# Two attentions first, then two feed-forwards over each quantised weight tile

## The chip, the cores and the metric

The kernel runs on one core of one Trainium2 chip. A core has TensorE (PE, matrix products), VectorE (DVE), ScalarE (ACT), GpSimd (POOL) and SyncE (SP), which here only issues DMAs; each has a queue of its own and works through it in order. The metric is the device time of one execution in microseconds, the median of several runs.

## The reference

One layer over an input of 4 x 1024 rows of 512 float32 values:

```python
# x: (4, 1024, 512)
x = x + layernorm(attn(layernorm(x), W_qkv, W_out))
x = x + layernorm(ffn(layernorm(x), w_gate_up, w_proj))

# attn: 16 heads of 32, element by element
q, k, v = split(x @ W_qkv.T); q, k = elu(q) + 1, elu(k) + 1
out = q * cumsum(k * v) / (q * cumsum(k) + 1e-9)        # sums along the 1024 rows
attn = out @ W_out.T * 32 ** -0.5

# ffn: both weights ternary: groups of 64, scale = mean|w|, w = round(w / scale) clipped to -1..1, times scale
h = silu(x @ Wgate.T) * (x @ Wup.T)                      # 2048 wide
ffn = rms_norm(h) @ Wproj.T
```

The straight-through form `w + (w_hat - w)` is computed in bfloat16 and its rounding is kept.

## The kernel before, in words

The 4096 rows are cut into 8 chunks of 512 (N); two chunks make a batch element, and an odd chunk takes its running sums (`carry`) from the even one. Attention and its weights work in float32 split in a high and a low part (`_hi`, `_lo`), three products per group of 4 x 128 rows of depth, 12 matmuls each: `group(s, g)` for g = 0 to 11 gives q, k and v of the four head tiles j (g = 3j + part), and `project_att(s, t)` projects the attention's result. The hidden layer has 16 tiles m of 128 (MT): `gate_up(f, m)` is 16 matmuls, `project(f, k)` adds hidden tile k into four banks with 8 matmuls, three tiles behind (LAG).

All engines run the same schedule, each written out by hand in its own block, and they meet at semaphores. `start()` does chunk 0 and 1's attentions, all weight preparation and the feed-forward of chunk 0. After it `step(s)` does the attention of chunk s and the feed-forward of chunk s - 1: 12 groups, the transposes of the normalised x1 (L470), 16 gate and up tiles with projections, then in `close` the transposes of the next chunk (L424) and the attention's output projection (L532). Steps 2 to 5 are a loop with a register (`run_steps`), 6 to 8 are written out.

Attention on the other engines, for a head tile j: ScalarE makes relu and exp (`features`, L737, L738), DVE combines them (L1087, L1089), multiplies k by v (L1097) and makes two running sums (L1106, L1109), together `front`. POOL (`numden`, L897 to L902) makes denominator and numerator, DVE the reciprocal (L1120, `back_reciprocal`), the quotient (L1128, `back_output`) and, after ScalarE's high part (L745), the low part (L1134, `back_lo`).

In the feed-forward, for a tile m: ScalarE applies silu (L768), DVE multiplies by the up product (L1171, `hidden_value`), ScalarE takes the high part (L779), DVE the remainder (L1176, `hidden_lo`), ScalarE squares (L785) and POOL adds the squares (L933, `add_square`).

The quantised weights come in 24 batches (BATCHES), 16 of gate and up rows ("gu") and 8 of the projection. A batch is 128 x 1024 and passes: load of two halves (SP, L358, three buffers), cast to bfloat16 (ACT, L692), `scale` (DVE, L1003 to L1011: sums of magnitudes, scale, reciprocal), `divide` (POOL, L866, four parts), `ternary` (DVE, L1030, L1032: clip and round), `scale_back` (POOL, L873, four parts), `diff` (DVE, L1038), from batch 13 on `total` (DVE, L1044), `transpose_weights` (PE, L447) into banks 2 and 3, and `put` (ACT, L701 and L704). PE turns weight and difference, 16 small matmuls, or from batch 13 (SUMMED) the one total, 8. Every two "gu" batches `row_scales` makes powers of two by masks on the exponent. `beside(m)` says which batches are turned beside tile m of chunk 0's feed-forward: seven are done before it, one per tile after that, two at tile 11. In this feed-forward gate and up have one bank each (`single=0`).

The order around a tile in `start()` on DVE is, for example, `hidden_value(0, m)`, `diff(b + 1)`, `hidden_lo(0, m)`, `total(b + 1)`, `ternary(b + 2)`, `scale(b + 3)`, and on POOL

```python
add_square(0, m)
for b in beside(m):
    scale_back(b + 2), divide(b + 3)
```

## Time and profile before

| | us |
|---|---|
| median of 3 runs | 1216.65 (1215.43 to 1217.48) |
| the profiled execution | 1217.18 |
| its span in the trace | 1215.0 |
| PE busy | 1107.6 (91%) |
| DVE busy | 808.3 (67%) |
| POOL busy | 555.6 (46%) |
| ACT busy | 444.5 (37%) |

The busy shares are over the whole span; the page also gives them in 40 slices of 30 us, in tenths:

```profile
PE   6859747877999999999989999999999999899997
DVE  6999989984787358843786268744785278535423
POOL 2856787784543424442442434342544253215322
PEclk9889888988999999999999999999999999999999
```

The first ten slices are `start()`, and the rest are steps. PEclk is the granted TensorE clock in tenths of full speed, 9 being 90% or more. A line of the timeline gives start, duration, engine, line, operation, output <- input, and in brackets how long the engine sat idle before and who released it.

### The profile page before, as it was taken

To read this page: it belongs to the slowest core of one execution; us is meant where nothing else is said; L and a number is where in the kernel's file an instruction comes from. 1 tells how busy PE (TensorE), PEld (TensorE's weight loads), DVE (VectorE), ACT (ScalarE), POOL (GpSimd) and SP (SyncE) were. 2 spreads that over 40 slices of the span, in tenths; PEclk is the share of its full clock that TensorE was granted. 3 is DMA by queue.
4 is the path that set the end of the run, shared out by engine and by line. 5 is a ranking of instruction groups with operands and counts; after the bars stand their busy time and mean duration, and the time that the engine had idled before them with its cause. 6 is when DMAs were issued, how large, how long until landed. Compare 5 with 4: busy or idle time off the path is not lost. (4 is left out here: it accounts for less than half of the span.)

```text
span 1215.0 us, 15144 instructions
## 1 busy us (share of the span) xinstructions
PE 1107.6 (91%) x5288; PEld 656.4 (54%) x5288; DVE 808.3 (67%) x1243; ACT 444.5 (37%) x754; POOL 555.6 (46%) x612
## 2 busy tenths in 40 slices
PE   6859747877999999999989999999999999899997
PEld 5648523334854477446844486446844585454443
DVE  6999989984787358843786268744785278535423
ACT  4423444543244323342234323441344314433432
POOL 2856787784543424442442434342544253215322
PEclk9889888988999999999999999999999999999999
DMA  7301121210210021000210021000200020100000
GB/s 253 102 1 53 36 68 45 95 44 1 70 35 1 1 70 35 1 1 2 71 35 1 1 70 35 1 1 10 90 6 1 1 70 1 35 1 1 35 1 35
DMA packets 28026, 42.92 MB, mean 35 GB/s; under 512 B 1328, under 2 KB 9520, under 8 KB 27952
## 3 DMA queue, kind: packets, MB, share of 16 engines
q1 hardware_dynamic: 27952, 41.95, 10.5%
q8 instruction: 45, 0.74, 0.2%
q14 instruction: 29, 0.24, 0.1%
HBM read 33.55 MB, written 8.39 MB: 35 GB/s over the span
## 5 line engine op out<-in xcount | busy, mean ns | idle before, releaser
L487 PE MATMUL bank<-x3t,wgu_t 128*128 128x512 f16 x1792 | 412.7, 384 | 28.1 <-DVE ht L1171 14.6
L487 PEld LDWEIGHTS bank<-x3t,wgu_t 128*128 128x128 bf16 x1792 | 173.8, 99 | 248.2 <-DVE ht L1171 20.2
L933 POOL TENSOR_TENSOR acc<-acc,ht 128x512 f32<-128x512 f32 x120 | 152.7, 1273 | 329.1 <-ACT ht L785 328.9
L494 PE MATMUL bank<-wproj_t,hid 128*128 128x512 bf16 x1024 | 242.2, 382 | 7.9 <-DVE tr L1097 7.5
L459 PE MATMUL bank<-xnt,wqkv_hi 128*128 128x512 f32 x768 | 196.6, 399 | 9.9 <-DVE tr L1097 9.4
L1171 DVE TENSOR_TENSOR ht<-ht,bank 128x512 f32<-128x512 f32 x128 | 86.5, 676 | 172.9 <-PE bank L487 135.6
L494 PEld LDWEIGHTS bank<-wproj_t,hid 128*128 128x128 f16 x1024 | 100.4, 98 | 128.8 <-DVE tr L1097 8.0
L459 PEld LDWEIGHTS bank<-xnt,wqkv_hi 128*128 128x128 f32 x768 | 146.2, 192 | 40.3 <-issue 10.3
L779 ACT ACTIVATE hid<-ht 128x512 f16<-128x512 f32 x128 | 80.5, 629 | 214.1 <-DVE ht L1171 214.1
L1176 DVE TENSOR_TENSOR hid<-ht,hid 128x512 f16<-128x512 f32 x128 | 105.8, 827 | 71.6 <-ACT hid L779 71.5
L785 ACT ACTIVATE ht<-ht,grow 128x512 f32<-128x512 f32 x120 | 86.6, 722 | 124.4 <-DVE hid L1176 124.4
L897 POOL TENSOR_TENSOR tk<-tq,ts 128x512 f32<-128x512 f32 x32 | 64.9, 2027 | 133.2 <-DVE ts L1106 133.2
L1120 DVE RECIPROCAL tk<-tk 128x512 f32<-128x512 f32 x32 | 106.9, 3340 | 10.5 <-POOL tk L900 10.5
L459 PE MATMUL bank<-xnt,wqkv_lo 128*128 128x512 f32 x384 | 104.4, 394 | 0.0
L768 ACT ACTIVATE ht<-bank 128x512 f32<-128x512 f32 x128 | 74.8, 585 | 31.7 <-PE bank L487 31.6
L459 PEld LDWEIGHTS bank<-xnt,wqkv_lo 128*128 128x128 f32 x384 | 73.5, 191 | 15.7
L532 PE MATMUL bank<-wout_hi,outt 128*128 128x512 f32 x256 | 69.6, 404 | 4.4 <-DVE outt L1134 4.4
L737 ACT ACTIVATE tr<-bank 128x512 f32<-128x512 f32 x32 | 19.2, 598 | 134.6 <-PE bank L459 121.9
L745 ACT ACTIVATE outt<-tr 128x512 fp32r<-128x512 f32 x32 | 19.9, 623 | 109.6 <-DVE tr L1128 109.6
L487 PE MATMUL bank<-x3t_last,wgu_t 128*128 128x512 f16 x256 | 57.5, 379 | 0.0
L532 PEld LDWEIGHTS bank<-wout_hi,outt 128*128 128x128 f32 x256 | 48.2, 190 | 15.6 <-issue 4.9
L879 POOL TENSOR_TENSOR vecf<-vecf,columns 128x4 f32<-128x4 f32 x8 | 8.1, 1018 | 80.5 <-DVE vecf L1060 80.5
(166 smaller groups left out, 1323.6 us busy)
## 6 DMA issues: line engine op xcount, KB each, us to landing
raw_q<-in_L_ffn_w_gate_up_dram SPq DMA_DIRECT2D x32, 256.0 KB, 2.8
xn<-in_L_attn_x_dram SPq DMA_DIRECT2D x7, 1024.0 KB, 5.1
x<-in_L_attn_x_dram SPq DMA_DIRECT2D x7, 1024.0 KB, 6.3
out_dram<-xn SPq DMA_DIRECT2D x7, 1024.0 KB, 8.7
raw_q<-in_L_ffn_w_proj_dram SPq DMA_DIRECT2D x16, 256.0 KB, 2.9
raw_a<-in_L_attn_W_qkv_dram SPq DMA_DIRECT2D x4, 768.0 KB, 9.1
xn<-in_L_attn_x_dram SPq DMA_DIRECT2D x4, 256.0 KB, 3.7
raw_out<-in_L_attn_W_out_dram SPq DMA_DIRECT2D x1, 1024.0 KB, 13.1
```

Of the source, the lines that this page charges most:

```text
L459: last = pe.matmul(bank[:], w[:, k, rows], xnt[:, part_x, k], start=(n == 0), stop=(n == 3 * KD - 1))
L487: last = pe.matmul(bank[:], wgu_t[:, k, first_row:first_row + P], x[:, part, k], start=(n == 0), stop=(n == 2 * KD - 1))
L494: last = pe.matmul(ps[4 + t][:], hid[:, part, k % HR, t * P:(t + 1) * P], wproj_t[:, k], start=(k == 0 and part == 0), stop=(k == MT - 1 a ...
L532: last = pe.matmul(bank[:], outt[:, part_o, k, t * P:(t + 1) * P], w[:, k], start=(n == 0), stop=(n == 3 * KD - 1))
L768: act.activation(ht[:, m % 2], ps[gate_bank(single, m)][:], ACT.Silu, scale=1.0 / SCALE3).then_inc(silu_done, 1)
L779: act.activation(hid[:, 0, m % HR], ht[:, m % 2], ACT.Copy).then_inc(h_hi, 1)
L785: act.activation(ht[:, m % 2], ht[:, m % 2], ACT.Square, scale=grow[:, m:m + 1]).then_inc(sq_done, 1)
L897: pool.tensor_tensor(tk[:, d], tq[:, d], ts[:, d], ALU.mult).then_inc(den_mul, 1)
L933: pool.tensor_tensor(acc[:], acc[:], ht[:, m % 2], ALU.add).then_inc(acc_done, 1)
L1120: dve.reciprocal(tk[:, d], tk[:, d]).then_inc(rec_done, 1)
L1171: dve.tensor_tensor(ht[:, m % 2], ht[:, m % 2], ps[gate_bank(single, m) + 1][:], ALU.mult).then_inc(h_done, 1)
L1176: dve.tensor_tensor(hid[:, 1, m % HR], ht[:, m % 2], hid[:, 0, m % HR], ALU.subtract).then_inc(h_lo, 1)
```

## The change

Only `start()`, what it calls and the storage are changed; steps 3 to 8 do the same work in the same order, but for one thing: three of the groups of step 3 are done ahead (AHEAD), and the steps are all written out.

- The attentions of chunks 0 and 1 are done first, both to the end: chunk 1's output projection is no longer beside the third chunk's.
- Of the weight batches only 0 and 1 are turned before the first gate. Batches pass a ring of 6 places that lies on freed attention storage (RING); divide and scale are four batches ahead of the turning, scale back and ternary two.
- The feed-forwards of chunks 0 and 1 run together: tile m of chunk 0 and tile m - 4 of chunk 1 (BEHIND). Tiles 0 to 3 of chunk 0 stand alone, one batch each; tiles 4 to 15 have two batches (m even) or one (m odd); then four tiles of chunk 1 alone with the transposes of chunk 2. The gate and up products of both rotate over three banks (`UNIT_AT`), and all turned halves go through bank 3.
- Chunk 0's projections are four tiles behind. Chunk 1's hidden tiles are all kept (`hid_b`), and their projections are done in `attention_of_third`: eight of them before the groups of chunk 2, the others one behind each of the first eight groups.
- Chunk 1's x1 is stored to the output's place in DRAM and loaded back later. The load of chunk 3's x waits for the store of chunk 0.
- Nothing is summed any more (`total` and SUMMED go); every batch is turned with 16 small matmuls. `row_scales` makes the power of two by float arithmetic, five dependent operations instead of three.

```diff
-        BEFORE = 7
-        SUMMED = 13
-        TWICE = (11,)
...
+        TURNED = {0: [2], 1: [3], 2: [4], 3: [5]}
+        for m in range(BEHIND, MT):
+            n = TURNED[m - 1][-1] + 1
+            TURNED[m] = [n, n + 1] if m % 2 == 0 else [n]
...
+        UNITS = []
+        for m in range(MT + BEHIND):
+            for f, n in ((0, m), (1, m - BEHIND)):
+                UNITS += [(f, n, which) for which in range(2) if 0 <= n < MT]
+        UNIT_AT = {unit: i for i, unit in enumerate(UNITS)}
+
+        def unit_bank(f, m, which):
+
+            return ps[UNIT_AT[f, m, which] % 3]
...
         def run_steps(eng, step):
-            with eng.Fori(1, NC // 2 - 1) as i:
-                step(2 * i, Step(2))
-                step(2 * i + 1, Step(3))
-            for s in range(NC - 2, NC + 1):
+            for s in range(3, NC + 1):
                 step(s, Step(s))
...
+            sp.wait_ge(y_ready, NT)
+            sp.wait_ge(kept_x1, 16)
+            sp.dma_start(x1[:], out_ch[1]).then_inc(back_x1, 16)
+            sp.dma_start(out_ch[0], xn[:]).then_inc(stored, 16)
+            sp.wait_ge(stored, 16)
+            sp.dma_start(xn[:], x_ch[3]).then_inc(x_loaded, 16)
...
+            def transpose_half(b, i):
+                kind, m = BATCHES[b]
+                turned = ident_b[:]
+                if i == 0:
                     pe.wait_ge(q_diff, b + 1)
...
+                    pe.wait_ge(q_out, 2 * b + i)
...
+                    for part, w in enumerate(PLACES[b]):
+                        last = pe.matmul(ps[3][:, n * P:(n + 1) * P], w[:, cols], turned, start=(part == 0), stop=(part == 1))
...
+            def attention_of_second():
...
+                    group(1, g, start=True)
+                    if g == 6:
...
                             project_att(0, t)
...
+                pe.wait_ge(ln2_x, NT)
+                transpose_x1(0, lambda k: None)
+                pe.wait_ge(att_hi, 2 * KD)
+                pe.wait_ge(att_lo, 2 * KD)
+                for t in range(NT):
+                    wait_group_read(pe, 1, 8 + t)
+                    project_att(1, t, ps[4 + t])
...
+                for m in range(BEHIND, MT):
+                    first, last = TURNED[m][0], TURNED[m][-1]
+                    project(0, m - BEHIND)
+                    unit(0, m, 0)
+                    transpose_half(first, 0)
+                    unit(0, m, 1)
+                    if last > first:
+                        transpose_half(first, 1)
+                    unit(1, m - BEHIND, 0)
+                    transpose_half(last, int(last == first))
+                    unit(1, m - BEHIND, 1)
+                    if last > first:
+                        transpose_half(last, 1)
...
+            def attention_of_third():
...
+                square_sums(0)
+                half = range(MT // 2)
+                for k in half:
+                    wait_hid(1, k)
+                    for t in range(NT - 1):
...
+                        project_tile(1, k, t)
...
+                square_sums(1, NT)
+                pe.wait_ge(ss_read, 2)
+                for k in half:
+                    project_tile(1, k, NT - 1).then_inc(FF_SECOND["pr_done"], 1)
+                for g in range(NG):
...
+                    group(2, g, start=True)
+                    k = MT // 2 + g
+                    if k < MT:
+                        wait_hid(1, k)
+                        for t in range(NT):
+                            last = project_tile(1, k, t)
...
+                for k in range(KD):
+                    wait_group_read(pe, 2, 8 + k)
+                transpose_x(3, bank=lambda k: ps[4 + k])
...
+                for g in range(AHEAD):
+                    group(3, g)
...
+                for t in range(NT):
+                    pe.wait_ge(fin_x, at(NT, 1, t))
+                    project_att(2, t)
...
+                for m in range(BEHIND, MT):
+                    first, last, n = TURNED[m][0], TURNED[m][-1], m - BEHIND
+                    hidden_gate(1, m), put_half(first, 0), hidden_hi(1, m)
+                    if last > first:
+                        put_half(first, 1)
+                    hidden_gate(2, n), put_half(last, int(last == first)), hidden_square(1, m), hidden_hi(2, n)
+                    if last > first:
+                        put_half(last, 1)
+                    hidden_square(2, n)
+                    for b in TURNED[m]:
+                        turn_and_cast(b)
...
+                for m in range(BEHIND, MT):
+                    b = TURNED[m][0]
+                    scale_back_and_divide(b)
                     add_square(0, m)
...
+                    if TURNED[m][-1] > b:
+                        scale_back_and_divide(b + 1)
+                    add_square(1, m - BEHIND)
...
+            def tile(s, j):
+
+                d = (s, j + 1) if j < KD - 1 else (s + 1, 0)
+                back_reciprocal(s, j)
+                front_features(*d), front_products(*d, True)
+                back_output(s, j)
+                front_sums(*d, d[0] % 2 == 1)
+                back_lo(s, j)
...
+                for m in range(BEHIND, MT):
+                    n, b = m - BEHIND, TURNED[m][0]
+                    hidden_value(0, m)
+                    if b + 1 < NBATCH:
+                        diff(b + 1)
+                    hidden_lo(0, m)
+                    if b + 2 < NBATCH:
+                        ternary(b + 2)
+                    hidden_value(1, n), scale_from(b + 4), hidden_lo(1, n)
+                    if TURNED[m][-1] > b:
+                        diff(b + 2)
...
+                            ternary(b + 3)
+                        scale_from(b + 5)
```

## Rows read from the trace of the kernel before

**Rows 1.** Busy time by stretch: us, engines' busy (instructions), granted clock, DMA.

```profile
0.00:145.08 145.08, 108.84 (x560) 88.77 (x561) 129.90 (x196) 53.49 (x103) 89.02 (x118) 0.92 0.27 89
145.08:297.17 152.09, 108.30 (x562) 50.29 (x561) 127.44 (x194) 70.11 (x128) 120.01 (x155) 0.88 0.17 54
312.52:445.52 133.00, 131.37 (x617) 77.72 (x616) 84.53 (x130) 47.61 (x78) 52.23 (x51) 1.00 0.08 24
219.82:243.33 23.51, 19.25 (x103) 8.57 (x101) 21.56 (x34) 12.35 (x23) 20.67 (x27) 1.00 0.38 124
```

**Rows 2.** The same for POOL lines L866, L873 and L933, in this order.

```profile
219.82:243.33 23.51, 10.59 (x12) 1.00 0.38 124
219.82:243.33 23.51, 6.44 (x12) 1.00 0.38 124
219.82:243.33 23.51, 3.83 (x3) 1.00 0.38 124
```

**Rows 3.** Timeline of PE: start, us, line, operation.

```profile
78.79 3.75 PE L459 MATMUL bank<-xnt,wqkv_hi 128*128 128x512 f32 x8 [9.38 <-DVE tr L1097]
...
293.27 0.61 PE L447 MATMUL bank<-ident_b,yq_own 128*128 128x128 bf16 x8
...
400.81 3.62 PE L487 MATMUL bank<-x3t,wgu_t 128*128 128x512 f16 x16
...
406.00 3.62 PE L487 MATMUL bank<-x3t,wgu_t 128*128 128x512 f16 x16
...
445.52 1.98 PE L459 MATMUL bank<-xnt,wqkv_hi 128*128 128x512 f32 x8
...
448.25 1.98 PE L459 MATMUL bank<-xnt,wqkv_hi 128*128 128x512 f32 x8
```

**Rows 4.** Timeline of DVE in the start and in step 2.

```profile
27.07 2.48 DVE L995 TENSOR_TENSOR wout_lo<-bank,wout_hi 128x512 fp32r<-128x512 f32 x4 [0.42 <-ACT wout_hi L682]
...
304.47 2.48 DVE L1051 BATCH_NORM_STATS2 stf<-bank 128x6 f32<-128x512 f32 x4
...
318.06 0.69 DVE L1087 SCALAR_TENSOR_TENSOR tq<-tq,tr 128x512 f32<-128x512 f32 x1 [3.66 <-ACT tq L738]
...
336.95 1.22 DVE L1106 TENSOR_TENSOR_SCAN ts<-columns,tk 128x512 f32<-128x512 f32 x1
...
341.21 3.35 DVE L1120 RECIPROCAL tk<-tk 128x512 f32<-128x512 f32 x1 [1.74 <-POOL tk L900]
...
348.80 0.68 DVE L1087 SCALAR_TENSOR_TENSOR tq<-tq,tr 128x512 f32<-128x512 f32 x1
...
350.79 1.22 DVE L1106 TENSOR_TENSOR_SCAN ts<-columns,tk 128x512 f32<-128x512 f32 x1
```

**Rows 5.** Waits of PE in step 2: us in total, times, longest.

```profile
PE bank L487 <- ACT ht L768: 1.6, 2, 1.2
```

**Rows 6.** Timelines of DVE (first two) and POOL, single operations.

```profile
195.17 0.68 DVE L1128 TENSOR_TENSOR tr<-tq,tk 128x512 f32<-128x512 f32 x1
...
196.38 0.42 DVE L1030 TENSOR_SCALAR yq_xn<-yq_xn 128x1024 bf16<-128x1024 bf16 x1
...
209.25 2.32 POOL L866 TENSOR_TENSOR yq_own<-wb_own,grs 128x256 bf16<-128x256 bf16 x4
...
228.11 3.67 POOL L866 TENSOR_TENSOR yq_set<-wb_set,grs 128x256 bf16<-128x256 bf16 x4
```

**Rows 7.** Groups of DVE lines from 219.82 to 243.33.

```profile
L1171 DVE TENSOR_TENSOR ht<-ht,bank 128x512 f32<-128x512 f32 x4 | 2.6, 650 | 0.0
...
L1176 DVE TENSOR_TENSOR hid<-ht,hid 128x512 f16<-128x512 f32 x3 | 2.9, 961 | 0.4 <-ACT hid L779 0.4
...
L1044 DVE TENSOR_TENSOR yq_own<-yq_own,wb_own 128x1024 bf16<-128x1024 bf16 x2 | 2.2, 1097 | 0.0
```

**Rows 8.** Waits of POOL from 219.82 to 243.33.

```profile
POOL yq_set L873 <- DVE yq_set L1032: 1.6, 2, 0.8
```

**Rows 9.** DMA issues: count, KB each, median us to landing.

```profile
out_dram<-xn SPq DMA_DIRECT2D x7, 1024.0 KB, 8.7
```

More of the change, by code:

```diff
@@ L416, in transpose_raw, with transpose_x @@
                     done.then_inc(wa_t, 1)
-            def transpose_x(c):
-                for k in range(KD):
+            def transpose_x(c, tiles=range(KD), bank=lambda k: ps[k]):
+                for k in tiles:
                     for t in range(NT):
@@ L458, in group @@
                     for k in range(KD):
-                        last = pe.matmul(bank[:], w[:, k, rows], xnt[:, part_x, k], start=(n == 0), stop=(n == 3 * KD - 1))
+                        last = pe.matmul(bank[:], w[:, k, rows], xnt_of(s)[:, part_x, k], start=(n == 0), stop=(n == 3 * KD - 1))
                         n += 1
@@ L471, in transpose_x1, with gate_up_unit, gate_up @@
                     last.then_inc(t3_done, 1)
-            def gate_up(f, m, single=MT, start=False, x=x3t):
-                for which, first_row, done in ((0, m * P, gate_done), (1, FF + m * P, up_done)):
-                    bank = ps[gate_bank(single, m) + which]
+            def gate_up_unit(bank, x, m, which):
+                first_row = which * FF + m * P
+                for n in range(2 * KD):
+                    part, k = divmod(n, KD)
+                    last = pe.matmul(bank[:], wgu_t[:, k, first_row:first_row + P], x[:, part, k],
+                                     start=(n == 0), stop=(n == 2 * KD - 1))
+                return last
+            def gate_up(f, m, single=MT, x=x3t):
+                q, c = ffn(f)
+                for which in range(2):
                     if m == 0 and which == 0:
@@ L481, in gate_up @@
                     if before >= 0:
-                        pe.wait_ge(h_done if which else silu_done, at(MT, f, before))
-                    if start:
-                        pe.wait_ge(q_out, 2 * (GU_AT[m] + 1))
-                    for n in range(2 * KD):
-                        part, k = divmod(n, KD)
-                        last = pe.matmul(bank[:], wgu_t[:, k, first_row:first_row + P], x[:, part, k],
-                                         start=(n == 0), stop=(n == 2 * KD - 1))
-                    last.then_inc(done, 1)
@@ L520, in square_sums @@
                     pe.wait_ge(x3t_lo, KD * (s + 1))
-                pe.wait_ge(acc_done, (MT - 1) * s)
-                for t in range(NT):
-                    last = pe.matmul(ps[3][:, t:t + 1], acc[:, t * P:(t + 1) * P], ones[:], start=True, stop=True)
-                last.then_inc(ss_done, 1)
+                square_sums(s - 1)
             def project_att(s, t, bank=None):
@@ L771, in hidden_parts @@
[L771 to L785 removed]
+                hidden_hi(s, m)
@@ L1283, in start @@
-                close(1, Step(1))
+                split_weights(4, 4 * KD)
+                front(0, 0, False, True), stats_x(1)
+                tile(0, 0), split_x(1), tile(0, 1), tile(0, 2), tile(0, 3), tile(1, 0)
+                stats_att(0)
+                back_reciprocal(1, 1), add_ln2(0), front_features(1, 2), front_products(1, 2, True)
+                back_output(1, 1), front_sums(1, 2, True), back_lo(1, 1)
+                stats_x1(0), scale(0), scale(1)
+                tile(1, 2), x3_lo(0), ternary(0), scale(2)
@@ new lines, in start @@
+                add_final(0)
+                read_square_sums(1, NT)
+                front(2, 0, False, True)
+                tile(2, 0), tile(2, 1), stats_x(3), tile(2, 2)
+                split_x(3, bank=lambda k: ps[4 + k])
+                stats("f", 1, lambda t: ps[t][:], before_second)
+                back_reciprocal(2, 3)
+                dve.wait_ge(back_x1, 16)
+                add_final(1, first_bank=0)
+                back_output(2, 3), back_lo(2, 3)
+                stats_att(2)
```

660 lines of the change are left out of this document (376 added, 284 removed).

## The prediction

> **What bounds the kernel now.** Read the page's busy shares first, then one line per stage: TensorE (PE) is busy for 131.4 of 133.0 us in the step from 312.52 to 445.52, at a granted clock of 1.00, but for 108.8 of the first 145.1 us and 108.3 of the next 152.1 us, at 0.92 and 0.88 [rows 1]. So after 297 us only PE's work counts, and before it some 80 us of PE time are empty. In those two stages VectorE (DVE) is busy 129.9 and 127.4 us; GpSimd (POOL) 120.0 us in the second. The reader is to see that the change can win in the first 300 us alone, and only as far as DVE and POOL can be spread over PE work.
>
> In the middle of the first feed-forward (219.82 to 243.33, three weight batches and three tiles) POOL is busy 20.7 of 23.5 us, DVE 21.6, PE 19.3 [rows 1]. POOL's lines there: dividing 10.59, scaling back 6.44, squares 3.83 us [rows 2]. One batch takes 23.51 / 3 = 7.84 us.
>
> The milestone for comparing: the moment when the third attention's output projection is done. Before, it ends at 445.52, where the next step's first of 12 groups starts [rows 3]. After, three of these groups are done by then: 12 matmuls take 448.25 - 445.52 = 2.73, 0.227 each, so they are 8.2 us, so PE is level at 445.5 + 8.2 = 453.7. But DVE counts too: it opened the step before this one at 318.06, 5.5 us after 312.52, held up by groups and activations [rows 4]; with three groups already there it opens 1.5 us after the milestone (my choice: its statistics' tail). DVE is level if the milestone comes at 451.0 - 1.5 = 449.5. PE waits in a steady step for 1.6 us only, at the first tiles, where DVE and ScalarE are late [rows 5], so the later of the two decides: level is 449.5.
>
> **Stage A, two attentions without quantisation.** Nothing up to the last weight split at 27.07 + 2.48 = 29.5 depends on what was moved [rows 4]. Then DVE alone: first head's front 5.0, statistics 3.1 (four of 0.6 and the small ones [rows 4]), first tile 9.2, split of x 2.4: 49.2. A tile in steady state: from the first scan's start to the reciprocal 341.21 - 336.95 = 4.26 (the 1.74 us of waiting for POOL's denominator in it stays, as nothing is left to fill it), reciprocal 3.35, output 0.7 [rows 6], features and product 350.79 - 348.80 = 2.0, less overlaps: 10.1 us [rows 4]. Bounds: 9.3 without any wait, 10.3 without overlap. The second tile's scan ends at 56.2, three more end at 86.4, tail 2.1: 88.5. Attention statistics, reciprocal, residual, the next head: 14.5, 103. Statistics 3.1, two scales 4.6, a tile 10, split of x3 2.4: 123. A list of 19 us (five parts of quantisation, reciprocal 3.35, output and split) puts the last attention split at 135, ternary(3) at 142. POOL's two divides and its denominator fit beside it. PE: 48 matmuls of 0.227 are 10.9 us, plus 2 for the slow clock after a long idle (8 matmuls took 3.75 instead of 1.98 us after 9.38 us idle, at 78.79 [rows 3]): 148. The two first batches then pass one bank by halves: four rounds of 8 small matmuls at 0.056 (0.45) [rows 3] and a copy of 0.6 with its hand-overs, 1.3 to 1.6 us each. First gate at 153.4. Before, it started at 145, but with two heads and an output projection still to do.
>
> **Stage B1, four tiles of the first chunk alone.** Four batches, second residual and its normalisation. DVE per tile and batch: 21.56 / 3 = 7.2 [rows 1], without the sum of 1.1 [rows 7] 6.1, and 0.3 more for the row scales (five dependent small operations where three were, every other batch): 6.4. Four of these, two statistics of 3.1, a residual 2.7, x3's remainder 2.4 and a first wait of 2 for the gates: some 38. POOL has four divides (3.5 each), four scalings (2.15), four squares, and 4.4 and 3.2 us for normalisation and residual: 39. End near 192. PE needs 17 us of this.
>
> **Stage B2, twelve iterations: two tiles, 1.5 batches and one projection each.** PE: 24 matmuls took 406.00 - 400.81 = 5.19, so 0.216 each [rows 3]; 32 + 8 of them 8.65, 24 small ones 1.35: 10.0 us. DVE: 2 x (0.65 + 0.96) = 3.2 for two tiles [rows 7], and 1.5 batches of 6.4 - 1.6 = 4.8: 10.4. POOL: 1.5 x (10.59 + 6.44)/3 + 2 x 1.28 = 11.1 [rows 2]. In 219.82 to 243.33 POOL's idle (2.8 of 23.5 us) is mostly the round divide - ternary - scale back (two of its three waits there are 1.6 us [rows 8]); the change puts divide four batches ahead instead of three, and this goes. But even iterations (two batches) cost POOL 13.9 and odd ones 8.2, where PE then sets 9.6; the queues let little slack pass (three rotating banks), so between 11.1 and (13.9 + 9.6)/2 = 11.8 I take 11.7. Bounds: PE's 10.0 below, 12.5 above (POOL keeping its wait of 0.93 per batch). Nine iterations until the divides run out: 105; normalisation of the third chunk 5 on POOL; three iterations at PE's pace 30. End 332 to 335. Four last iterations of one tile, projection and transpose: 22.7. End 357.5.
>
> The extra 8 small matmuls of the 11 batches whose halves are no longer summed (88 x 0.056 = 4.9 us of PE) stand under POOL's pace but for the last four batches (1.8); the sums' 11 x 1.1 us leave DVE, which is second. ScalarE has 12.35 us of work in 23.51 [rows 1], 4.1 per batch and tile, so at most 8.2 per iteration of 11.7: covered.
>
> **Stage C, third attention.** Split of the last x tile behind the last value: PE waits 1.5. Square sums 0.8, 24 pairs of projections 10.4, square sums and their read 1.2, 8 pairs 3.5: 17.4. Twelve groups of 2.72 and eight projections of 1.73 alternate to 63.8. DVE's third tile, behind the chunk statistics, gives its product at 68.8, and the transposes of the fourth chunk wait for it: 5 us. Transposes 2, split of x behind the tile's end at 72.7: groups start at 75.2, a 4 us wait. Three groups, partly at the slow clock, 84.5; DVE in that time statistics, reciprocal, final residual and the last head: 86.3. Projection 10.9: 97.2. (Bounds 88, if the split slips in early, and 101.) The fourth chunk's load comes after a store whose copies land 8.7 us after issue [rows 9]; x is due at 60 and the chain ends near 35: hidden.
>
> Milestone 357.5 + 97.2 = 454.7, 5.2 later than 449.5. The profiled span becomes 1215.0 + 5.2 = 1220.2; the execution took 1217.18, 0.5 more than the median of 1216.65, so 1216.65 + 5.2, rounded down for B2's choice near its upper bound: **1221 us**. Unrolling the loop gives nothing: the looped step from 312.52 to 445.52 already has PE at 131.4 of 133.0.
>
> **A rule weighed against the trace.** In the three batches above, DVE and POOL operations that touch both buffers slow each other: a divide of four parts takes 3.67 us, and 2.32 undisturbed [rows 6]. The Trainium skill (SBUF — State Buffer, "SBUF: two separate sides") says that the pair of ports shared by the two is held exclusively for a whole instruction, by a GpSimd operation or by a VectorE one with two SBUF inputs or in a two-port mode. Added up by that rule from undisturbed durations (POOL 2.32 + 2.32 + 1.27 = 5.9; DVE 0.85 for a ternary and three of 0.68, 2.9 [rows 6]) a batch would need 8.8 us, and the trace shows 7.84: the lock is real but doesn't cover whole durations.
>
> **Rivals.** (1) *PE's pace holds in B2.* If divides and ternaries shrink to undisturbed durations (1.5 x 4.64 + 2.6 = 9.5 us of POOL), the two queues slip past one another and an iteration is 10.0 to 10.3: 9 x 1.5 = 14 less, and B1 two less: 1205. For it: 2.32 us divides occur. Against it: DVE is at 10.4 itself, so they will meet. (2) *The shared port sums up.* By POOL 9.5 and DVE 1.5 x 1.53 + 2 x 0.68 = 3.7 us an iteration is 13.1: 9 x 1.4 = 13 more: 1234. Against it the 7.84. The skill's rule named above is this case. (3) *The start's waits chain.* The single bank for transposes ties PE, ScalarE and DVE in B1 and B2: every half waits for a copy, and a late difference stops the gates behind it on PE's queue; at 1 us per iteration this is 12 to 20 us: 1235. (4) *The third attention hides everything*, stage C at 88: 1212.
>
> **Chances.** Forecast 0.42, (1) 0.28, (2) and (3) 0.20, (4) 0.10. Against no change 0.2% (2.4 us) can just be told. The forecast's own spread is 1214 to 1228. Faster: (1), half of (4) and a little of the forecast, 0.36; within 0.2%: 0.13; slower 0.51. Range 1199 to 1238: it takes in (1) and (2) with PE's pace as lower bound.
>
> **What would show it.** Right: first gate at 151 to 156 with PE idle over 40 us before it; in the double feed-forward POOL at 93% or more, an iteration 11.3 to 12 us while divides last and near 10 after; PE waits of 4 to 6 us at the fourth chunk's transposes and again at its first group; the milestone near 455. Wrong: iterations at 10.3 or at 13, a first gate before 148, or steady steps from the fourth on that differ from 133 to 135 us.

## The result and the profile after

| | before | after |
|---|---|---|
| median, us | 1217.07 (1215.43 to 1217.83, 4 runs) | 1242.26 (1240.74 to 1243.59, 4 runs) |
| ratio | | 1.0208 (1.0191 to 1.0224) |
| the profiled execution | 1217.18 | 1242.10 |
| its span | 1215.0 | 1239.8 |

2.1% slower. The direction is that of the forecast, which gave "slower" 0.51, but 1221 us and even the range's end of 1238 are too low: the rise is 25 us instead of 5.

First the stretches of the changed kernel, cut at the first gate, the first of the twelve iterations, the end of the tenth, the end of the twelfth, the start of the third attention and the milestone (columns as in [rows 1]):

```profile
core 0: us, PE busy (x) PEld busy (x) DVE busy (x) ACT busy (x) POOL busy (x), PEclk, DMA share, GB/s
0.00:158.00 158.00, 112.25 (x528) 92.21 (x529) 133.71 (x208) 47.78 (x89) 78.14 (x101) 0.88 0.23 79
158.00:195.01 37.01, 24.54 (x148) 13.16 (x146) 28.10 (x51) 21.07 (x39) 27.03 (x41) 0.86 0.37 114
195.01:318.41 123.40, 100.77 (x575) 50.04 (x584) 89.32 (x160) 61.44 (x111) 95.71 (x128) 0.92 0.17 53
318.41:350.11 31.70, 29.84 (x182) 15.08 (x184) 21.82 (x28) 16.66 (x29) 24.35 (x29) 1.00 0.00 1
350.11:372.50 22.39, 22.34 (x110) 11.06 (x110) 7.33 (x11) 9.75 (x16) 6.01 (x5) 1.00 0.00 0
372.50:477.07 104.57, 86.46 (x385) 60.84 (x389) 58.55 (x90) 18.22 (x31) 29.10 (x31) 0.93 0.16 51
```

The third row is where to look. It holds nine iterations, each from the start of one projection to that of the next: 195.01, 207.3, 218.3, 235.4, 246.4, 263.2, 273.9, 290.9, 301.9, 318.41. That is 13.7 us each, and behind the first (12.3) about 17 and 11 in turn: the long ones turn two batches, the short ones one. No engine is full in them: PE 82%, POOL 78%, DVE 72%. In the middle of the first feed-forward POOL had 88% and DVE 92% [rows 1]. So no engine's work alone sets this pace; waits do. Here they are for the same stretch (engine, what waited, for whom: us in total, times, longest):

```profile
PE bank L486 <- ACT wgu_t L849: 21.6, 8, 4.8
ACT ht_b L956 <- DVE hid_b L1387: 20.2, 7, 4.4
DVE ht_b L1381 <- PE bank L516: 16.8, 5, 4.7
POOL yq L1054 <- DVE grs L1218: 14.8, 5, 4.7
POOL yq L1061 <- DVE yq L1246: 12.6, 5, 3.8
```

Each engine waits for another that itself waits, a ring. One such wait in order of time, DVE first (L1387 is `hidden_lo`, L1213 to L1221 `scale`, L1230 to L1238 `row_scales`):

```profile
219.87 0.67 DVE L1381 TENSOR_TENSOR ht_b<-ht_b,bank 128x512 f32<-128x512 f32 x1
220.47 1.21 DVE L1213 TENSOR_REDUCE grs<-wb 128x16 f32<-128x1024 bf16 x1
...
222.23 0.16 DVE L1230 TENSOR_TENSOR row_bound<-row_max 128x2 f32<-128x2 f32 x1
222.43 0.52 DVE L1232 TENSOR_SCALAR grow<-row_bound 128x2 f32<-128x2 f32 x1
222.99 0.53 DVE L1234 TENSOR_TENSOR shrink<-grow,row_bound 128x2 f32<-128x2 f32 x1
223.55 0.54 DVE L1236 TENSOR_TENSOR grow<-grow,shrink 128x2 f32<-128x2 f32 x1
224.12 0.17 DVE L1238 RECIPROCAL shrink<-grow 128x2 f32<-128x2 f32 x1
224.20 0.98 DVE L1387 TENSOR_TENSOR hid_b<-ht_b,hid_b 128x512 f16<-128x512 f32 x1
```

then ScalarE:

```profile
220.58 0.63 ACT L946 ACTIVATE hid_b<-ht_b 128x512 f16<-128x512 f32 x1 [1.38 <-DVE ht_b L1381]
225.22 0.72 ACT L956 ACTIVATE ht_b<-ht_b,grow 128x512 f32<-128x512 f32 x1 [4.01 <-DVE hid_b L1387]
225.85 1.13 ACT L841 ACTIVATE wb<-raw_q 128x512 bf16<-128x512 f32 x2
226.89 0.57 ACT L922 ACTIVATE ht<-bank 128x512 f32<-128x512 f32 x1
227.37 0.58 ACT L849 ACTIVATE wgu_t<-bank 128x512 bf16<-128x512 f32 x1
```

and TensorE:

```profile
221.98 1.89 PE L516 MATMUL bank<-x3t,wgu_t 128*128 128x512 f16 x8
228.00 0.29 PE L486 MATMUL bank<-diag,wb 128*128 128x128 bf16 x1 [4.13 <-ACT wgu_t L849]
```

The high part is there at 220.58 + 0.63 = 221.2. The remainder could follow, but DVE is in the scales of a batch four places ahead, until 224.2. ScalarE's square overwrites the value that the remainder reads, so it stands still for 4.01 us, and behind it in its queue are the cast, the next silu and the copy of a turned half. TensorE needs that copy, because all halves share bank 3, and stands still for 4.13 us. When it goes on, a small matmul takes 0.31 us instead of 0.22.

The third attention is longer too. PE, DVE and POOL around the transposes of the fourth chunk:

```profile
448.37 3.41 PE L466 MATMUL bank<-ident_f,xn 128*128 128x128 f32 x16 [11.46 <-DVE tr L1305]
455.12 3.52 PE L497 MATMUL bank<-xnt,wqkv_hi 128*128 128x512 f32 x8 [3.33 <-DVE xnt L1394]
```

```profile
435.94 0.17 DVE L1273 TENSOR_SCALAR vec<-mv 128x4 f32<-128x4 f32 x1
442.79 3.35 DVE L1328 RECIPROCAL tk<-tk 128x512 f32<-128x512 f32 x1 [6.69 <-POOL tk L1088]
```

```profile
436.18 1.01 POOL L1067 TENSOR_TENSOR vec<-vec,columns 128x4 f32<-128x4 f32 x1 [13.84 <-DVE vec L1273]
437.69 3.02 POOL L1077 TENSOR_SCALAR xn<-xn,vec 128x512 f32<-128x512 f32 x4 [0.22 <-POOL vec L1069]
440.68 1.26 POOL L1085 TENSOR_TENSOR tk<-tq,ts 128x512 f32<-128x512 f32 x1
```

POOL's queue has `norm_x(3)` ahead of `numden(2, 2)`. Its sums were ready at 431.2 (the scan at 429.99 takes 1.22), but POOL waits for the statistics of x until 436.18, after 13.84 us of idleness, and makes the denominator only at 440.68. DVE's reciprocal waits 6.69 us for it.

At the start, the second attention's output projection (L604) begins late:

```profile
140.24 2.05 PE L604 MATMUL bank<-wout_hi,outt_b 128*128 128x512 f32 x4 [22.59 <-issue]
```

```profile
134.44 0.69 DVE L1336 TENSOR_TENSOR tr<-tq,tk 128x512 f32<-128x512 f32 x1
135.04 1.21 DVE L1213 TENSOR_REDUCE grs<-wb 128x16 f32<-128x1024 bf16 x1
...
139.15 0.98 DVE L1342 TENSOR_TENSOR outt_b<-tr,outt_b 128x512 fp32r<-128x512 f32 x1
```

Between the output and its low part stand 4.1 us of `scale(3)` with its row scales.

Behind the milestone, 477.07, one wait is new (for VectorE's residual of the third chunk):

```profile
480.95 2.12 PE L497 MATMUL bank<-xnt,wqkv_hi 128*128 128x512 f32 x8 [1.00 <-DVE x L1357]
```

From there to the end it is 1239.8 - 477.07 = 762.7 us, and before 1215.0 - 453.7 = 761.3. So 23.4 of the 24.8 us lie ahead of the milestone.

### The profile page after: what moved, and what is told of

Same layout as the page of the kernel before. It is cut to its first block and busy times, and to the rows that moved or that the text cites. A ratio compares the mean times of both kernels' runs of the same rounds, so it can differ in the third digit from the quotient of the medians.

```text
span 1239.8 us, 14664 instructions
## 1 busy us (share of the span) xinstructions
PE 1110.7 (90%) x5315; PEld 663.7 (54%) x5376; DVE 793.0 (64%) x1248; ACT 442.6 (36%) x752; POOL 551.2 (44%) x612
## 5 line engine op out<-in xcount | busy, mean ns | idle before, releaser
L516 PE MATMUL bank<-x3t,wgu_t 128*128 128x512 f16 x1536 | 353.1, 383 | 11.6 <-ACT ht L922 7.9
L1137 POOL TENSOR_TENSOR acc<-acc,ht 128x512 f32<-128x512 f32 x105 | 134.7, 1282 | 275.4 <-ACT ht L956 275.2
L516 PEld LDWEIGHTS bank<-x3t,wgu_t 128*128 128x128 bf16 x1536 | 149.2, 99 | 195.3 <-ACT ht L922 12.8
L552 PE MATMUL bank<-wproj_t,hid 128*128 128x512 bf16 x840 | 202.6, 381 | 6.4 <-ACT x3t_b L907 3.5
L497 PE MATMUL bank<-xnt,wqkv_hi 128*128 128x512 f32 x672 | 170.5, 396 | 4.9 <-DVE xnt L1394 3.3
L497 PEld LDWEIGHTS bank<-xnt,wqkv_hi 128*128 128x128 f32 x672 | 126.4, 190 | 32.3 <-issue 4.3
L1387 DVE TENSOR_TENSOR hid<-ht,hid 128x512 f16<-128x512 f32 x112 | 91.5, 817 | 61.2 <-ACT hid L946 60.6
L1054 POOL TENSOR_TENSOR yq<-wb,grs 128x256 bf16<-128x256 bf16 x96 | 69.3, 751 | 18.6 <-DVE grs L1218 18.6
L1061 POOL TENSOR_TENSOR yq<-yq,gsc 128x256 bf16<-128x256 bf16 x96 | 56.9, 623 | 25.9 <-DVE yq L1246 25.9
L516 PE MATMUL bank<-x3t_b,wgu_t 128*128 128x512 f16 x256 | 66.0, 405 | 0.0
L604 PE MATMUL bank<-wout_hi,outt 128*128 128x512 f32 x192 | 53.3, 410 | 4.4 <-DVE outt L1342 4.4
## 6 DMA issues: line engine op xcount, KB each, us to landing
raw_out<-in_L_attn_W_out_dram SPq DMA_DIRECT2D x1, 1024.0 KB, 13.1
```

Of the source, the lines that this page charges most:

```text
L497: last = pe.matmul(bank[:], w[:, k, rows], xnt_of(s)[:, part_x, k], start=(n == 0), stop=(n == 3 * KD - 1))
L516: last = pe.matmul(bank[:], wgu_t[:, k, first_row:first_row + P], x[:, part, k], start=(n == 0), stop=(n == 2 * KD - 1))
L552: last = pe.matmul(bank[:], hid_of(f, part, k)[:, t * P:(t + 1) * P], wproj_t[:, k], start=(k == 0 and part == 0), stop=(k == MT - 1 and p ...
L604: last = pe.matmul(bank[:], outt_of(s, part_o)[:, k, t * P:(t + 1) * P], w[:, k], start=(n == 0), stop=(n == 3 * KD - 1))
L1054: pool.tensor_tensor(part(yq, i), part(wb, i), spread(grs[:, b % RING], i), ALU.mult).then_inc(q_y, 1)
L1137: pool.tensor_tensor(acc[:], acc[:], ht_of(f)[:, m % 2], ALU.add).then_inc(q["acc_done"], 1)
```

## The experiments

The theory, *the order of the queues*: each lost stretch is an instruction that stands ahead of a more urgent one in the order of one engine. Rivals: *POOL's work* (squares, divides), and *the shared port*. All times are medians; before ran beside them at 1215.8 to 1216.6, and ratios are to it. "Iteration" is the mean of the nine in that run's trace. A stage read from one trace can differ between executions of the same code: third_order's edit acts only in the third attention, but its trace has the first projection of the twelve at 192.78 and the changed kernel's at 195.01. So moments of two traces are compared only where the difference is above some 2 us, or where medians say the same.

### One move at a time, on the changed kernel

**third_order**

```diff
-                numden(2, 0), numden(2, 1), norm_x(3), numden(2, 2), numden(2, 3)
+                numden(2, 0), numden(2, 1), numden(2, 2), norm_x(3), numden(2, 3)
```

> Changed kernel with one move on POOL: the normalisation of chunk 3 (norm_x(3)) comes after numden(2, 2) instead of before it. Theory (part of the loss is POOL's queue in the third attention: VectorE's reciprocal of head 2 waited 6.7 us because POOL was held by a normalisation whose statistics came late): the reciprocal's wait falls to about 0.5 us, PE's idle before the fourth chunk's transposes from 11.5 to about 5.5 us, total 1242.3 - 6 = 1236. Rival (PE is slack there and is caught up later by VectorE): same time within 1 us.

1234.43, ratio 1.0144 (1.0127 to 1.0161): 7.8 us in the medians for one name moved. By the traces the third attention is 5.5 us shorter (370.9 to 469.94, 99.0 us, against 104.6); the milestone is 7.1 earlier, but 1.6 of that lie ahead of the third attention, where the edit changes nothing. DVE's reciprocal no longer waits, and PE's wait is halved (DVE, then PE):

```profile
435.24 3.35 DVE L1328 RECIPROCAL tk<-tk 128x512 f32<-128x512 f32 x1
```

```profile
440.81 3.65 PE L466 MATMUL bank<-ident_f,xn 128*128 128x128 f32 x16 [5.53 <-DVE tr L1305]
```

**narrow_squares**

```diff
+                    if f < 2:
+                        acc = acc[:, :1]
+                        pool.tensor_tensor(acc, acc, ht_of(f)[:, m % 2, :1], ALU.add).then_inc(q["acc_done"], 1)
+                        return
```

> Changed kernel, but POOL adds the squares of the first two feed-forwards over 1 column instead of 512, so these two sums of squares are left out. It takes about 1.1 us x 30 = 33 us of work from POOL. Theory (the double feed-forward is bound by waits that pass through ScalarE's and VectorE's queues, not by POOL's work): under 5 us faster, 1237 to 1242, an iteration of two tiles still 13 to 13.7 us. Rival (POOL's work and the port it shares with VectorE set the pace, as the prediction had it): nine iterations 2.2 us shorter each, 1242 - 20 = 1222.

1232.26, 1.0119 (1.0102 to 1.0135), iteration 13.1. 10.0 us are won for 31.7 us of POOL's busy time taken out (551.2 to 519.5). That is between the two expectations, under 5 and 20: POOL's work counts, for 5.8 us in the nine iterations (123.4 to 117.6), but they stay at 13.1 and it doesn't set their pace.

**lo_first**

```diff
-                    hidden_value(1, n), scale_from(b + 4), hidden_lo(1, n)
+                    hidden_value(1, n), hidden_lo(1, n), scale_from(b + 4)
```

> Changed kernel with one swap on VectorE in the double feed-forward: hidden_lo(1, n) before scale(b + 4) instead of after it and its row scales. Theory (chain of queues: ScalarE's square of the second chunk's tile waits for that remainder, and the next gate and the copies of turned weights wait behind the square): ScalarE's wait of up to 4.4 us per pair of iterations goes, VectorE pays 0.7 us per iteration for the high part; pairs of iterations fall from 28 to about 24.5 us, total 1242 - 14 = 1228. Rival (POOL bound): unchanged within 2 us.

1238.27, 1.0178 (1.0161 to 1.0195), iteration 13.1: 4.0 us, where 14 were expected. One iteration of its trace takes 20.0 us (265.12 to 285.07), the one in which DVE makes the statistics for chunk 2, and the tenth, where POOL has their normalisation, takes 16.1 instead of 9.8. The other eight of the nine take 12.2. POOL waits for the scales as long as before in the nine (14.5 us against 14.8).

**masks**

```diff
-                dve.tensor_scalar(power, bound, LEADING_BIT, None, ALU.mult).then_inc(q_bound, 1)
-                ...
+                dve.tensor_scalar(shrink[:].bitcast(I32)[:, pair], bits, EXPONENT, EXPONENT,
+                                  ALU.bitwise_and, ALU.bitwise_xor).then_inc(q_shrink, 1)
+                dve.tensor_scalar(grow[:].bitcast(I32)[:, pair], bits, EXPONENT, None, ALU.bitwise_and).then_inc(q_grow, 1)
```

> Changed kernel with the row scales of before: three small operations by masks on the exponent instead of five dependent float ones. Each of the eight calls took 2.1 us and should take 0.9. Theory (they stand in the chain): one in stage A on the way to the last attention split, five in the double feed-forward just before the remainder that ScalarE waits for: 6 x 1.1 = 6 us faster, 1236. Rival (VectorE has slack there, 72% busy): within 2 us of 1242.

1236.87, 1.0166 (1.0149 to 1.0183), iteration 12.7: 5.4 us for an edit that the prediction had priced at 0.3 us per batch. The trace is of the fastest of its four executions, 1233.06, so its iteration is somewhat too short for the median.

**act_late**

```diff
-                    hidden_gate(1, m), put_half(first, 0), hidden_hi(1, m)
+                    hidden_gate(1, m), put_half(first, 0)
+                    if m > BEHIND:
+                        hidden_square(2, n - 1)
+                    hidden_hi(1, m)
...
-                    hidden_square(2, n)
```

> Changed kernel with one move on ScalarE in the double feed-forward: the square of the second chunk's tile comes after the next iteration's gate and first copy of turned weights, no longer ahead of them. Theory (chain of queues): PE's waits for the copies (21.6 us in nine iterations) fall by half or more, 1242 - 10 = 1232 or lower. Rival (the bound is POOL's order, which now gets its square later): within 2 us of 1242 or slower.

1232.48, 1.0136 (1.0111 to 1.0161), iteration 12.3: 9.8 us, the most of any move inside the double feed-forward. In the nine iterations ScalarE's wait of 20.2 us for the remainder is 9.3, and PE's of 21.6 us for the copies is 8.8, as the theory had it. This shows the chain: the same work, with the blocked instruction no longer ahead of the copy.

**before_unrolled**, the kernel before with its steps written out:

```diff
-            with eng.Fori(1, NC // 2 - 1) as i:
-                step(2 * i, Step(2))
-                step(2 * i + 1, Step(3))
-            for s in range(NC - 2, NC + 1):
+            for s in range(2, NC + 1):
```

> The kernel before with nothing changed but the loop over steps 2 to 5 written out. The prediction gave this part of the change nothing: 1216.6 within 2 us. Rival (part of the loss is the fetching of a longer program): 3 us or more slower.

1215.32, 0.9994 (0.9984 to 1.0004): nothing, as forecast.

### Moves together

**all4** is third_order, lo_first and masks; **all5** adds act_late.

> third_order, lo_first and masks together in the changed kernel. If the three gains (7.9 from the third attention, 4.0 and 5.4 from the chain) are of different places they add up: 1242 - 17 = 1225. If lo_first and masks shorten the same stretch (the remainder that ScalarE waits for stood behind the row scales), their sum is nearer 6: 1229.

> The three of the run before and the later square of act_late. Chain theory: with the square out of the gate's way, the iterations near the 11.7 us that POOL's work allows, nine times 1.3 less than now: 1215 to 1222, level with the kernel before. Rival (once the remainder comes early the square waits for nothing, so its place no longer counts): same as without, 1225 to 1229.

1234.52 and 1234.31, both 1.0152 (1.0127 to 1.0177). Both were misses: third_order alone has 1234.43. Two iterations of all4 take 19.6 and 19.3 us, the first where DVE makes statistics for chunk 2, the second where POOL has their normalisation. PE and DVE in the second:

```profile
321.49 0.29 PE L487 MATMUL bank<-ident_b,wb 128*128 128x128 bf16 x1 [8.19 <-DVE yq L1249]
```

```profile
317.41 4.02 DVE L1249 TENSOR_TENSOR yq<-yq,wb 128x1024 bf16<-128x1024 bf16 x1 [3.50 <-POOL yq L1062]
```

Not all of the 8.19 us is order. DVE waits 3.50 for POOL's scaling back, which stands behind the normalisation, but then the difference itself takes 4.02 us, where others of its kind take 0.68. POOL works meanwhile without a gap, dividing from 317.34 to 319.66 and adding a square until 320.88, and the difference ends 0.55 us after that. So some 3.3 us of this wait look like the port that the two engines share; no run tried it by itself.

**late_norm_lo** is all4 with the two moved; **three** is third_order, masks and act_late; **four** is three with the two moved:

```diff
-                    if m == 11:
+                    if m == 14:
                         norm_x(2)
...
-                    if m == 9:
+                    if m == 13:
                         stats_x(2)
```

> The kernel all4 with the statistics of chunk 3's input (the third chunk) four tiles later and its normalisation three tiles later. In all4 one iteration of the double feed-forward took 19.3 us: PE waited 8.2 us for a difference on VectorE, which waited for POOL, whose scaling back stood behind that normalisation. Theory (this ate what lo_first and masks gave): that wait goes and the four small gains add up, 1234.5 - 9 = 1225. Rival (the stall only moves): 1232 or more.

> third_order, masks and act_late together, VectorE's order as in the change. Theory (in the changed order scale, row scales and the remainder stand one behind the other; the masks shorten it and the late square takes it out of ScalarE's way): gains 7.9 + 5.4 and half of act_late's 9.8, 1242.3 - 18 = 1224. Rival (as in all4 a normalisation on POOL eats them): 1232.

> The kernel three with the late statistics and normalisation of the third chunk. Theory (queues, no engine's work): nine iterations at 12 us, 1220 or a little less, level with the kernel before (1216.6) or up to 4 us slower; the other 5 us of stage A and what is lost in tiles 0 to 3 stay. Rival (statistics later hold up the tail): as three or slower.

late_norm_lo: 1227.09, 1.0087 (1.0070 to 1.0103), 7.4 less than all4. three: 1225.26, 1.0075 (1.0058 to 1.0092). four: 1216.68, 1.0007 (0.9994 to 1.0020). The edits of four, none of which takes away work beyond two of the five operations of 128x2 in each row scale, bring the whole loss back; its nine iterations take 102.7 us, 11.4 each.

**four_narrow**, four with narrow_squares, asks whether POOL's work sets that pace.

> The kernel four, but with the squares of the first two feed-forwards added over 1 column only, so these two sums are left out; 33 us less work on POOL. It tells what bounds the double feed-forward once the chain is shorter. If POOL's work is the bound then (11.1 us per iteration by its lines, now 9.0): 15 us or more faster than four. If it is still the chain: 5 to 10 us, as the 10.0 that the same cut gave before.

1202.92, 0.9886 (0.9870 to 0.9903), iteration 10.3: 13.8 us for 32.3 us of POOL's busy time (557.7 to 525.4), against 10.0 on the changed kernel: nearer to the 15 expected of POOL's bound than to the 5 to 10 of a chain. Once the order is mended, the rival of POOL's work comes mostly true; the 10.3 is near PE's own 10.0, so the run can't show a pace of POOL's below that.

### The start, and the last long iteration

**split_first**, on the changed kernel:

```diff
-                back_reciprocal(1, 3), ternary(1), back_output(1, 3), scale(3), back_lo(1, 3)
+                back_reciprocal(1, 3), ternary(1), back_output(1, 3), back_lo(1, 3), scale(3)
```

> The changed kernel with one move on VectorE in the start: the scales of the fourth batch, scale(3) with its row scales (135.04 to 139.15 in the changed kernel's trace), come behind the last attention split back_lo(1, 3) instead of ahead of it. Theory (the second attention's output projection, which began at 140.24 after TensorE's idle 22.6 us, hangs on that split alone): the projection begins 3 to 3.5 us earlier, near 137, the first gate near 155, and the time falls by 2.5 to 3.5 us, to about 1239. Rival (the batches' divides, which wait for the same scales, then come late and stop the first gates instead): the first gate stays within 1 us of 158.0 and the time within 1 us of 1242.3.

1237.71, 1.0174 (1.0159 to 1.0190): 4.6 us, more than expected. The output projection begins at 136.94 instead of 140.24, the first gate at 155.6 instead of 158.0, the first projection of the twelve at 189.5 instead of 195.0; of this last difference 2 us are as likely one execution against another.

**four_later** is four with `stats_x(2)` at 14 and `norm_x(2)` at 15; **five_moves** adds split_first; **six_moves** adds lo_first to that.

> The kernel of the four moves (1216.7) with the statistics of the third chunk one iteration later, at m == 14 instead of 13, and its normalisation at m == 15 instead of 14. Theory (at m == 13 the statistics of 4.2 us stand ahead of the last batch's difference on VectorE, and that stretch of 16.2 us with TensorE waiting 5 us for the difference and again for a copy is what is left of the order's cost): the 16.2 us become 11 to 12, and 4 to 5 us are won, but the normalisation, now later, may cost 1 to 2 at the first split of the third chunk: 1212 to 1214. Rival (the iteration is long because a divide-and-scale round is late in any case): no gain, 1216 to 1218.

> The kernel of the four moves with the later statistics and normalisation of the third chunk and with the last attention split ahead of the fourth batch's scales: both edits of the two runs above. Theory (the waits are at different places, before 158 and behind 296 us, with full queues of work between them): the gains add to 6 to 8 us: 1209 to 1211, faster than the kernel before by 0.5%. Rival (GpSimd's work from the first divide to the last square sets this stretch, and the divides don't start earlier): the second edit gives nothing here, 1212 to 1214.

> The kernel of the run before with one more move: hidden_lo(1, n) ahead of scale_from(b + 4) on VectorE. Theory (this shortens the tile of the chunk behind by one scale and row scales, but it delays the scales on which GpSimd's divides wait, and GpSimd is now over 90% busy): no gain or a loss of 1 to 4 us against the run before. Rival (the tile's wait is still the one that TensorE feels): a gain of 2 to 4 us, as it gave alone on the changed kernel (4.0).

four_later: 1223.65, 1.0053 (1.0040 to 1.0067). five_moves: 1220.62, 1.0035 (1.0023 to 1.0047), 3.0 less. six_moves: 1226.28, 1.0079 (1.0065 to 1.0093). The first was a miss in sign, and with it the second's 1209 to 1211: the long iteration falls from 16.2 to 11.3 us, but the normalisation now stands behind the squares of tile 15, and PE waits for it in four_later:

```profile
336.06 0.30 PE L467 MATMUL bank<-ident_f,xn 128*128 128x128 f32 x1 [3.21 <-POOL xn L1081]
336.72 0.33 PE L467 MATMUL bank<-ident_f,xn 128*128 128x128 f32 x1 [0.36 <-POOL xn L1081]
```

lo_first, which won 4.0 us alone, loses 5.7 here, and POOL's waits for the scales in the nine iterations go from 3.2 us in five_moves to 10.3: with POOL near its bound, a late scale is dearer than a late remainder.

**stats_alone** is four with `stats_x(2)` at 14 and `norm_x(2)` left at 14; **best** adds split_first.

> The kernel of the four moves (1216.7) with the third chunk's statistics at m == 14 instead of 13, and the normalisation left at m == 14. In the run with both one later the iteration behind the statistics fell from 16.2 to 11.3 us, but the normalisation (3.02 us on GpSimd from 335.14) stood behind the squares of m == 15, one of which waited 1.6 us, and TensorE's first transposes of the third chunk came 6.6 us late. Theory (these two are separate: 4.9 us won by the statistics, 6.6 lost by the normalisation): with the normalisation at 14 the iteration stays at 11.3 and the four last ones take their 22 to 23 us: 1212 to 1213. Rival (the normalisation at 14 waits for the later statistics on GpSimd, with the squares behind it, and stops the tiles): 1216 to 1220.

> The kernel of the run before with the last attention split ahead of the fourth batch's scales. Alone on the changed kernel this gave 4.6 us, on top of the later normalisation 3.0. Theory (the first gates and GpSimd's first divides both follow from the earlier projection): 3 us less than the run before, 1209 to 1210, faster than the kernel before by 0.5%. Rival (GpSimd's work swallows it): no difference between the two.

stats_alone: 1216.46, 1.0006 (0.9996 to 1.0015). best: 1213.54, 0.9987 (0.9978 to 0.9996). Both came out some 4 us above their expectation. stats_alone's trace has the long iteration at 11.3 us and its milestone at 451.25 against four's 456.98, yet the medians differ by 0.2 us. Two of four's ten executions took 1221.26 and 1222.09, the other eight 1214.74 to 1217.32, and the profiled one is the first of the two: the 16.2 us are probably theirs alone, and the usual execution had nothing there to win. This isn't shown, since the eight left no trace. best is 2.9 us below stats_alone, the 3 that split_first was to give; it beats the changed kernel by 2.2% (1.0208 / 0.9987), and the kernel before by 0.13%; its interval ends below 1, but this is less than the 0.2% that the prediction took as tellable. The same nine iterations in best:

```profile
191.20:293.10 101.90, 92.30 (x576) 46.55 (x585) 90.72 (x139) 60.44 (x112) 93.97 (x119) 1.00 0.21 66
```

with PE's wait for the copies and ScalarE's for the remainder:

```profile
ACT ht_b L957 <- DVE hid_b L1387: 5.3, 4, 1.9
PE bank L487 <- ACT wgu_t L850: 5.3, 8, 1.3
```

Set against the third row of after, 123.40 - 101.90 = 21.5 us are gone. PE's idle time went from 22.6 to 9.6, that is 13.0, and its busy time for the same matmuls from 100.8 to 92.3, that is 8.5, at a granted clock of 1.00 instead of 0.92. POOL is busy 92% of the time. That DVE and POOL slow each other isn't what the mended order cured. Such slowing is in their busy times, and these are no lower here: 90.7 and 94.0 us against 89.3 and 95.7, which hold 3.3 us of statistics and 4.8 of normalisation that best does behind the nine.

## Why the prediction failed, step by step

| step | forecast | measured | difference |
|---|---|---|---|
| A, first gate | 153.4 | 158.0 | +4.6 |
| B1, four tiles alone | 38 | 37.0 | -1.0 |
| B2, twelve iterations | 143.4 | 155.1 | +11.7 |
| four last iterations | 22.7 | 22.4 | -0.3 |
| C, third attention | 97.2 | 104.6 | +7.4 |
| milestone | 454.7 | 477.1 | +22.4 |
| level point | 449.5 | 452.3 | -2.8 |
| span against before | +5.2 | +24.8 | +19.6 |

B2's forecast is what its times leave: 357.5 - 22.7 - (153.4 + 38). The stages are measured in one trace each. The measured level point is no reading of its own: it is 477.1 less the 24.8 us of the spans.

- **What bounds the kernel.** Right: the steps behind the milestone kept their pace (762.7 us against 761.3), and win or loss lay in the first 300 us of before with PE's empty 80. DVE as the later one at the level point was a mis-sized term: the wait that it causes is 1.0 us, not the 4.2 between 453.7 and 449.5. The rest takes 1.4 us longer than before, so level is 1.4 ahead of PE's 453.7, at 452.3.
- **Stage A.** The tiles' pace of 10.1 us was nearly right: DVE's reciprocals start at 50.20, 60.50, 70.82 and 81.25, 10.3 to 10.4 apart. The last split, put at 135, ended at 140.1, but "a list of 19 us" isn't what was mis-sized: from the end of x3's split to it the forecast has 12 us (123 to 135) and the trace 12.05 (128.08 to 140.13). The 5.1 us came before, a little in each term: the split put at 49.2 ended at 50.3, the 88.5 were 91.2, the 103 were 106.8, the 123 were 128.1. The projection and the four rounds behind it took 17.8 us instead of 18.4. What the forecast overlooked is another thing: it counted the list as work that DVE has to do before the split, but `scale(3)` had no need to be there. split_first gives 4.6 us for that, much the same number by chance.
- **Stage B1.** Right as a sum of DVE's and POOL's work. PE, put at 17 us, was busy for 24.5 there, at a granted clock of 0.86; it isn't the bound.
- **Stage B2, the step that failed.** I compared the engines' work (10.0, 10.4, 11.1) and took "11.7 with the queues letting little slack pass". The work was right: with the order mended, four, stats_alone and best run at 11.3 to 11.4, POOL at 92%, and four_narrow points to POOL as what sets it. What failed is the 0.6 us that stood for the queues (11.7 less 11.1): it measured 2.4 (13.7 less 11.3). What I left out is that DVE, ScalarE and PE each have their instruction of the one tile ahead of the next, so the scales delay the remainder, the square, the copy and the turning in a row. It cost 2.0 us per iteration above the forecast, 2.4 above the mended order; 0.9 of this is PE's longer busy time at the lower granted clock. Most of the loss is in the even iterations, about 17 us against the 13.9 of POOL's work; the odd ones took 11 against 9.6. The forecast for the whole of the twelve is less wrong than its nine (123.4 against 105) because the third chunk's normalisation, put at 5 us behind them, took place inside them: the rest took 31.7 us instead of 35 to 38.
- **The four last iterations** at PE's pace: right within 0.3.
- **Stage C.** The 4 us wait at the first group was right (3.33); the 5 us at the transposes was 11.46. I let DVE's third tile follow behind "the chunk statistics" and overlooked that POOL's list has the normalisation ahead of that tile's denominator. third_order leaves 5.53 us there, the forecast's wait, and makes the stage 5.5 us shorter in its trace. What is left, 99.0 us against 97.2, is mostly the transposes, which took 3.65 us instead of 2. The late load of the fourth chunk was hidden: its statistics at 433.03 waited for no DMA.
- **Unrolling**: nothing, shown by before_unrolled.
- **The rivals.** (3), waits that chain, came nearest to the true mechanism: the one bank for the turned halves is a link of the ring. But it named the bank and a late difference, and the traces show late instructions ahead of urgent ones in the queues of DVE and ScalarE, with the bank as it was in every run; a second bank wasn't tried. I had put it at 1 us per iteration and at a chance it shared with (2); it was 2, and the two other queue orders came on top. (2), the shared port, forecast 13.1 us per iteration and the trace has 13.7, but this agreement is by chance: but for two small operations less, the same DVE and POOL work takes 11.3 in best, with busy times no lower. As a sum of durations the port's price fails here as it did at 8.8 against 7.84 us per batch; that the two engines slow each other is seen again (below). (1), PE's pace, comes only with POOL's squares cut out: 10.3 in four_narrow. (4) fell with stage C.

## What to carry to other kernels

When two streams of work are put side by side on engines that work in order, busy times bound the pace from below only. Walk each queue with the question: what stands ahead of this instruction, when is that one ready, and who waits for me? Above all look at instructions that are ready late (statistics, a square behind a remainder) ahead of ones on which another engine hangs. Try moves together as well as alone: 7.8, 5.4 and 4.0 us became 7.7 in all4, and lo_first changed its sign once another engine was the bound.

## What the runs showed of the hardware

- Some small DVE operations take three times as long beside POOL's. On 128x2, three of them take 0.52 to 0.54 us each (222.43, 222.99 and 223.55, in the rows above) and two 0.16 and 0.17. POOL meanwhile divides in four parts of 0.58:

```profile
222.32 2.32 POOL L1054 TENSOR_TENSOR yq<-wb,grs 128x256 bf16<-128x256 bf16 x4
```

  Its parts end at 222.90, 223.48 and 224.06, and the three operations at 222.95, 223.52 and 224.09: each seems to wait for the end of one part. The row agrees with the rule of the Trainium skill (SBUF — State Buffer, "SBUF: two separate sides") that a GpSimd instruction keeps the shared ports for its whole length. The reciprocal at 224.12, beside the fourth part, takes 0.17 us and doesn't wait; by the same section only VectorE operations with two SBUF inputs or in a two-port mode need these ports; a reciprocal has one input, and in which mode it ran no trace shows. Over all eight pairs of batches the five operations take 15.3 us of DVE's time (by line: 1.7, 3.8, 4.2, 4.3 and 1.3), 1.9 a pair; the three of before took 7.6 (2.2, 4.2 and 1.2). The prediction priced the difference at 0.3 per batch, 0.6 a pair, and it is 1.0. The longest such case is the difference of 4.02 us in all4. The port wasn't tried by itself.
- The clock makes waits dearer. Behind the 4.13 us at 228.00 a small matmul takes 0.31 us and not 0.22, and the nine iterations of after lose 8.5 us of PE time to a granted clock of 0.92. In best, where PE waits 2.4 us just ahead of the first projection and at most 1.3 at a time after it, it is 1.00.
